# Early matmuls on ones, the index vector by another queue, and weights issued behind two stores

## The reference

```
x: 32 x 64 x 1024, itok: 32 numbers from 0 to 15, cond_w: 16 x 64 x 64
y   = einsum('bct,bcd->bdt', x, cond_w[itok])          condition product
h   = gelu(y @ w1 + b1)        w1: 1024 x 4096         first product
out = x + h @ w2 + b2          w2: 4096 x 1024         second product
```

## Time and profile before

| | us |
|---|---|
| three timed runs | 1264.7, 1264.99, 1266.15 |
| median | 1264.99 |
| profiled execution | 1264.25 |
| its span, first to last instruction | 1262.4 |
| PE busy | 1255.4 (99%) |
| DVE, ACT, POOL busy | 832.3, 567.3, 184.0 |

### The profile page before, as it was taken

How to read it: one execution, slowest core, us unless ns; L and a number is a source line. 1 busy time by engine, 2 the same in 40 slices (tenths; PEclk the granted TensorE clock), 3 DMA queues, 4 the chain that set the end, 5 groups by cost and what they waited for, 6 DMA issues and landing times.

```text
span 1262.4 us, 15333 instructions
## 1 busy us (share of the span) xinstructions
PE 1255.4 (99%) x5645; PEld 1042.8 (83%) x5645; DVE 832.3 (66%) x1087; ACT 567.3 (45%) x969; POOL 184.0 (15%) x94
## 2 busy tenths in 40 slices
PE   9999999999999999999999999999999999999998
PEld 8878888888888888888888888888888888888887
DVE  5978678676477767657566555555547777784764
ACT  4745545454544444444434444444445444444442
POOL 3342233311000000000034233222300000000000
PEclk9999999999999999999999999999999999999999
DMA  9596656673998322249835235553189932322431
GB/s 350 149 318 233 211 215 243 250 266 134 375 395 296 100 101 100 94 145 378 307 131 187 104 122 184 184 183 131 74 331 399 349 134 98 100 100 98 155 131 51
DMA packets 95084, 249.54 MB, mean 198 GB/s; under 512 B 8322, under 2 KB 16546, under 8 KB 93602
## 3 DMA queue, kind: packets, MB, share of 16 engines
q1 hardware_dynamic: 93922, 248.28, 54.3%
q10 hardware_dynamic: 1088, 0.28, 0.1%
HBM read 162.55 MB, written 85.98 MB: 197 GB/s over the span
## 4 chain that ended last, share of the span: by engine, by line
PE 96%; DVE 2%; DMA 1%; issue 0%; ACT 0%; POOLq 0%; SPq 0%; ACTq 0%; DVEq 0%
PE ps L568 48%; PE ps L552 46%; PE ps L497 1%; PE ps L512 1%; DMA y_mem<-y_out 1%; DVE y_whole L785 1%; DMA cond_all<-in_L_cond_weights_dram 0%; DVE lhs L790 0%; DVE acc L868 0%; ACT lhs L636 0%; DVE y_whole L772 0%; DVE y L779 0%; DVE y_out L895 0%; DVE hs L804 0%; ACT y_stage L613 0%
## 5 line engine op out<-in xcount | busy, mean ns | idle before, releaser
L552 PE MATMUL ps<-y,lhs 128*128 128x512 f32 x2688 | 611.6, 389 | 1.4 <-ACT c L642 1.2
L568 PE MATMUL ps<-rhs,lhs 128*128 128x512 f32 x2688 | 609.6, 389 | 0.0
L552 PEld LDWEIGHTS ps<-y,lhs 128*128 128x128 f32 x2688 | 503.9, 188 | 106.5 <-ACT c L642 1.6
L568 PEld LDWEIGHTS ps<-rhs,lhs 128*128 128x128 f32 x2688 | 504.5, 188 | 104.8
L706 ACT ACTIVATE lhs<-h_raw 128x512 fp32r<-128x512 f32 x224 | 141.7, 632 | 345.8 <-PE ps L568 340.2
L849 DVE TENSOR_TENSOR lhs<-h_raw,lhs 128x512 fp32r<-128x512 f32 x224 | 155.2, 693 | 188.4 <-ACT lhs L706 188.4
L790 DVE TENSOR_TENSOR lhs<-w_raw,lhs 128x512 fp32r<-128x512 f32 x128 | 112.6, 881 | 124.6 <-ACT lhs L636 124.5
L636 ACT ACTIVATE lhs<-w_raw 128x512 fp32r<-128x512 f32 x128 | 81.0, 633 | 166.8 <-PE ps L552 162.9
L852 DVE TENSOR_TENSOR rhs<-W,rhs 128x512 fp32r<-128x512 f32 x224 | 153.4, 685 | 0.0
L790 DVE TENSOR_TENSOR lhs<-s_w,lhs 128x512 fp32r<-128x512 f32 x96 | 90.1, 940 | 88.0 <-ACT lhs L636 87.8
L715 ACT ACTIVATE rhs<-W 128x512 fp32r<-128x512 f32 x224 | 137.9, 616 | 0.0
(11 more groups left out here) (37 smaller groups left out, 299.9 us busy)
## 6 DMA issues: line engine op xcount, KB each, us to landing
h_raw<-h_mem SPq DMA_DIRECT2D x112, 512.0 KB, 3.3
w_raw<-in_L_ffn_inter_w_dram SPq DMA_DIRECT2D x32, 1024.0 KB, 8.9
h_mem<-hs SPq DMA_DIRECT2D x64, 512.0 KB, 4.6
W<-in_L_ffn_output_w_dram SPq DMA_DIRECT2D x32, 1024.0 KB, 12.7
h_mem<-c SPq DMA_DIRECT2D x48, 512.0 KB, 5.7
y_mem<-y_out SPq DMA_DIRECT2D x28, 512.0 KB, 3.1
y<-y_mem SPq DMA_DIRECT2D x7, 2048.0 KB, 12.9
acc<-in_x_dram SPq DMA_DIRECT2D x16, 512.0 KB, 8.2
```

The costliest lines, as they stand in the source:

```text
L552: last = nc.tensor.matmul(ps[:, bank, :], w[:, k, :], y[i][:, part, k, :], start=(i in FRESH and k == 0 and u == 0), stop=(k == KH - 1 and ...
L568: last = nc.tensor.matmul(ps[:, bank2(h, j, tb), :], lhs[s % RING][:, a, blk(tb)], rhs[r][:, w, :], start=(j in FRESH and q == 0 and u == ...
```

## The change

Four things. The matmuls ahead of the condition product are no longer 11 of 128 x 512 in float32r on zeros, but 10 and, behind the product with b1, 3 more of 128 x 128 in float32 on ones. itok is loaded through ACT's queue, between cond_w's half and b1, and no longer as SP's first transfer. A group's weights are issued within `keep_rest`, behind the stores of hs1 and c11, and no longer ahead of them; this holds for groups 2 to 7 of both passes. The second bias b2 is issued in group 2, behind its stores, and no longer ahead of group 1.

```diff
-    WARM = 11
+    WARM = (10, 3)
-        zeros = at("zeros", 96, [BANK], F32R)
+        ones = at("ones", 96, [2 * P])
@@ keep_rest(h, g)
                 keep(h, 0, g, c11, c11_kept)
                 if g == NG - 1:
                     load_h(h, HRING)
+                elif g + 2 < NG:
+                    load_w1(h, g + 2)
                 sp.wait_ge(hs_made[2], n)
@@ SP
-            sp.dma_start(itok_sb[0:1], itok.rearrange("(o b) -> o b", o=1)).then_inc(itok_in, 16)
             sp.dma_start(cond_all[0:C], cond_w.rearrange("s c d -> c s d")).then_inc(cond_in, 16)
...
-            sp.dma_start(b2_all[:], b2.partition_broadcast(P)).then_inc(b2_in, 16)
...
-                    if g + 1 < NG and (h, g) != (0, 0):
-                        if (h, g) == (1, 0):
-                            sp.wait_ge(out_kept[0], 16)
-                            sp.wait_ge(out_kept[1], 16)
-                        load_w1(h, g + 1)
+                    if (h, g) == (1, 0):
+                        sp.wait_ge(out_kept[0], 16)
+                        sp.wait_ge(out_kept[1], 16)
+                        load_w1(1, 1)
                     if g > 0:
                         keep_rest(h, g - 1)
+                    if (h, g) == (0, 2):
+                        sp.dma_start(b2_all[:], b2.partition_broadcast(P)).then_inc(b2_in, 16)
@@ PE
+            def warm(count):
+                for i in range(count):
+                    nc.tensor.matmul(ps[:, i % 2, 0:P], ones[:, 0:P], ones[:, P:2 * P], start=True, stop=True)
-            pe.wait_ge(zeros_made, 1)
-            for i in range(WARM):
-                nc.tensor.matmul(ps[:, i % 2, :], zeros[:, 0:P], zeros[:], start=True, stop=True)
+            pe.wait_ge(ones_made, 1)
+            warm(WARM[0])
             pe.wait_ge(b1_in, 16)
             pe.wait_ge(ident_made, 1)
             nc.tensor.matmul(ps[:, 7, 0:F // P], b1_rows[0:F // P], ident[0:F // P], start=True, stop=True).then_inc(b1_turned, 1)
+            warm(WARM[1])
@@ ACT
             act.dma_start(cond_all[C:P], cond_w.rearrange("s c d -> c s d")).then_inc(cond_in, 16)
+            act.dma_start(itok_sb[0:1], itok.rearrange("(o b) -> o b", o=1)).then_inc(itok_in, 16)
@@ DVE
-            nc.vector.memset(zeros[:].bitcast(F32), 0.0).then_inc(zeros_made, 1)
+            nc.vector.memset(ones[:], 1.0).then_inc(ones_made, 1)
```

More of the change, by code:

```diff
@@ L129, in build @@
         out_done = sem("out_done")
-        zeros_made = sem("zeros_made")
+        ones_made = sem("ones_made")
         wdiag_zero = sem("wdiag_zero")
```

## The result

Twenty runs each: before 1264.11 us median (1262.81 to 1266.15), changed 1267.61 us (1265.18 to 1269.89). The ratio is 1.0024, 95% interval 1.0016 to 1.0031. Forecast was 1262.9 with a range to 1264.6. Single executions of either kernel spread over 3 to 5 us, so medians are compared, and traces are read for where a hole stands, not for tenths of the total. The changed kernel's twenty times form two groups of ten, 1265.18 to 1266.89 and 1268.33 to 1269.89; the median lies in the gap between them (the means of the two kernels are 3.0 us apart), and the one trace is of the upper group.

What follows compares the result with a forecast made beforehand. It took PE, busy 99% of the span, as the bound, so only holes could be won. From the profiled 1264.25 us, -0.35 (opening) and -1.0 (group 1) gave 1262.9 us; range for 8 in 10: 1261.2 to 1264.6.

Steps and rivals of the forecast that it cites:

- What bounds the kernel: Whole span: PE is busy 99%, so only holes or slow stretches can be won, about 4.2 us or 0.33%.
- the c11 hole: Group 1, 88.74 us: PE's 1.42 us hole goes, as c11's store lands at 81.7, before ACT wants it at 82.80.
- the chain behind it: Group 1: from y_out's landing through ACT, DVE and POOL to PE's next start takes 8.6 us.
- The cap on the clock's gain: Step at 38 us: DVE's y_sum waits for POOL's sum, so of 1.8 us from an early clock none passes.
- The gain that the prediction let through: Step at 38 us: PE starts 0.35 us earlier, because POOL's picks come 0.35 us earlier.
- y_out's landing in group 1: The y_out store lands at 92.9, or 93.2 with DMA engines briefly empty, instead of 94.2; PE restarts at 101.85.
- group 1 gave -1.0 in the forecast: Group 1: of 1.92 us in two holes 1.0 us is taken back, some 0.9 us stays; bounds 0 and 1.92.
- Rival 2: Group 1: the hole only moves, y_out's store lands at 94.2, PE restarts at 102.84; 1263.9 us, chance 0.18.
- "nothing" in groups 2 to 6: Later weights and a fuller queue ahead of y_out cost nothing; bounds -0.2 and +0.3 us in each of three groups.
- Rival 4: Groups 3, 4 and 6: the late weights burst blocks y_out, 3 us a group, 1272 us in all; chance 0.05.
- the opening: Start to the step at 38 us: 0.35 us gained; bounds 0 and 2.2 us.
- the spread: Runs' median lies 0.74 us above the profile, read as later clock rises; early products shield, so no surcharge expected.

Runs made afterwards that it cites:

- w_first: Kernel before with the weights behind two stores only once, in group 1 of the first pass; 1266.43 us, ratio 1.0024.
- p_ones: Kernel before with only the early products changed, to 10 and 3 on ones in the condition product's shape; 1263.21 us, ratio 0.9997.
- p_weights: Kernel before with only the weights moved, behind the stores of hs1 and c11 in both passes; 1269.55 us, ratio 1.0045.
- w_first_nobias: w_first with the second bias issued in group 2, that is the changed kernel's group 1 alone; 1266.76 us, ratio 1.0024.
- p_itok: Kernel before with only itok moved to ACT's queue; 1263.39 us, ratio 1.0002.
- no_weights: Changed kernel with the weights where they were before; itok, early products on ones and bias still moved; 1263.21 us, ratio 1.0002.
- w_three: p_weights with a third buffer for y_out and the bias loaded in group 7; 1264.55 us, ratio to before 0.9999.
- w_behind_y: Kernel before with bias in group 2 and, in first-pass groups 1 to 6, weights behind six stores and three y_out stores; 1267.78 us, ratio 1.0037.
- b1_first: no_weights with b1 issued ahead of itok on ACT's queue; 1262.69 us, ratio to before 0.9989.
- p_bias: Kernel before with only the second bias moved, to group 2; 1263.62 us, ratio 1.0005.
- y_three: Kernel before with three y_out buffers and the bias in group 7, weights where they were; 1262.50 us, ratio 0.9990.
- best: Kernel before with three y_out buffers, bias in group 7, early products on ones, itok behind b1 on ACT's queue; 1262.91 us, ratio 0.9994.

## Why the prediction was wrong, step by step

**Right.** What bounds the kernel, and that the c11 hole goes: c11's store no longer holds ACT (0.25 us for 5.29). That the hole then belongs to y_out's store, by the chain behind it: from landing to PE 8.6 us before and in the changed kernel 96.85 to 105.48, 8.6 us again. The cap on the clock's gain: in eleven of the traces the first product starts between 21.8 and 22.4 us, over a microsecond earlier than before, and the step at 38 us still starts between 38.35 and 38.85 (before 38.45), with PE idle 1.3 to 1.9 us. The wait is the one named, DVE's y_sum beside POOL's sum, here in w_first:

```profile
23.16 2.40 POOL L468 TENSOR_TENSOR s_w<-w_raw 128x1024 f32<-128x1024 f32 x1 [0.92 <-DMA w_raw<-in_L_ffn_inter_w_dram]
23.97 3.81 DVE L788 TENSOR_TENSOR y_whole<-y_whole,y_whole 128x1024 f32<-128x1024 f32 x2
```

DVE's two sums start 1.1 us earlier than before (25.05) and are through at 27.8 instead of 27.7 us. The gain that the prediction let through, 0.35 us, is nearer to 0. It was to come from earlier picks, behind which POOL starts its sum. But in nine of the eleven traces POOL has done its picks and waits, as in this row, until 23.0 to 23.5 us for the first weights to land, a wait that the prediction did not have. In p_ones the chain of waits runs by these weights as well, through DVE's pieces lhs, and y_sum starts only at 24.74.

**Wrong, the term that decided: y_out's landing in group 1, put at 93.2.** It was 96.9, of which 0.75 us is the late start and 2.9 us the step. I had queued the same bytes at the 406 GB/s of the earlier trace rows and allowed 0.3 us for empty engines. The windows show 207 GB/s from 77 to 79 us and 325 from 79 to 87 in the changed kernel:

```profile
77.00:79.00 2.00, 2.00 (x10) 1.65 (x10) 1.93 (x4) 1.52 (x3) 0.00 (x0) 1.00 0.52 207
79.00:87.00 8.00, 8.00 (x37) 6.63 (x36) 7.12 (x10) 3.71 (x7) 0.00 (x0) 1.00 1.01 325
```

At 406 that is 0.4 + 0.65 MB or 2.6 us not moved. A rate read from one order of transfers was carried to another. So group 1 gave -1.0 in the forecast and +1.9 in the trace. Rival 2's sign came, ACT let go later than 94.2, but its hole did not only move, it grew. Which property of the order lowers the rate stays open.

**Wrong: "nothing" in groups 2 to 6.** The same step, bounded at +0.3 us for each of three groups; measured were 0.98 and 0.84 us in two of them, and 0.7 and 1.3 us in p_weights. Rival 4 named this mechanism, place (groups 3, 4, 6) and sign, and I gave it 0.05, because its price was worked out for a full 5.2 us of delay and its condition (the burst not drained at 165.6) from the same 406 GB/s. Where a rival's condition rests on the same number as the forecast, it is not independent of it; its chance should have been that of the number being wrong.

**Left out: what a hole does to the clock.** The prediction priced a hole at its length. Behind holes of 2.5 to 3.3 us in group 1 the clock fell in three traces (w_first, w_first_nobias, p_weights) and cost 1.6 to 1.7 us more. The changed kernel's trace escaped it; whether its other executions did no run shows.

**Wrong: the opening, put at -0.35.** It was +0.74 in the trace. The bound 0 to -0.42 left out that itok's issue occupies ACT's queue for 1.0 us ahead of b1 (b1 issued at 2.59 instead of 1.53, landed 5.0 us later instead of 4.0). It also left out that ACT's half of cond_w lands after 6.1 us instead of 3.6 when SP's stream of cond_w and x starts earlier (5.1 to 6.1 us in the five traces with that start); that the two share the DMA engines is a reading. The expectation "PE now takes its product right behind the early stream" fell with it, by an idle time of 2 us, and the clock is at 1.2 GHz behind that. In medians this part is small: p_itok and no_weights are not told from before.

**Half right: the spread.** I read the 0.74 us between profile and median as later rises of the clock. The traces show the clock up or down ahead of the condition product in executions of both kinds of early product, on zeros too (p_itok, p_weights, w_first: 14.53 us), and a fall behind the hole at 38 us in p_ones for 1.6 us. But the early products do not shield from that: in p_ones they made the hole in which it falls. And a part of the spread has nothing to do with the clock. In 15 of the 18 traces the span ends 4.6 to 4.7 us after the last stores of the result begin to be issued, in three (p_weights, w_three, w_behind_y) 6.5 to 6.7 us; those two microseconds lie behind PE's last product. p_weights' longer span (1269.5 us) holds them, w_three's too.

## What to carry to other kernels

When a transfer is moved behind others, the waits that it used to precede get it in front of them: list every store that a waiting engine needs and count what is issued ahead of it in the new order, and do not take the rate of the old order for the new. If two waits stand one behind the other, take away the wait with a further buffer (5.0 us here) rather than reorder what feeds it. An early clock on an engine that then waits for two others was worth nothing here. Price a hole not by its length alone: the clock can fall behind it, which cost another 1.6 us.

## What the runs showed of the hardware

- The column of the granted clock reads 1.00 at the very start although records there take 0.2 us instead of 0.11; once the clock has been up and falls, it reads 0.50 to 0.54 (9 to 12 us in the changed kernel, 38.6 to 41.9 us in p_ones, 99.2 to 102.6 us in w_first, w_first_nobias and p_weights).
- PE's clock fell to 1.2 GHz behind idle times of 1.2 (with 0.5 more shortly after, b1_first), 1.6 (p_bias), 1.8 (p_ones), 1.9 (y_three), 2.0 (the changed kernel) and 2.5 to 3.3 us (w_first_nobias, w_first, p_weights). It did not fall behind 1.3 to 1.9 us at the step at 38 us in ten traces, nor behind 2.56 us in the changed kernel's group 1. So the length alone does not decide.
- Sixteen DMA engines at a busy share of 1.01 moved 311 to 329 GB/s over 8 us, and 413 at 1.05, with the same kinds of transfer in another order.
- A one-row transfer of 128 bytes, second on ACT's queue, kept that queue for 0.77 to 1.01 us in three traces (no_weights, p_itok, the changed kernel); as SP's first it took 0.36 us, as ACT's third 0.53 us. b1's 16 KB in the second place took 0.67 us, 0.92 us in `best`.
- In 3 of 18 traces the span ends 2 us later behind the last stores than in the others. In these two microseconds the DMA share is 0.03 to 0.06 (12 to 18 GB/s), about what one of the 16 engines alone would show (1/16 is 0.06); in before and w_first it is 1.02 and then 0.5 in the same two microseconds ahead of the end.
